# Dividing attention's sums dim-major: sums and denominators moved by DMA instead of turned on TensorE

## The chip, the cores and the metric

The kernel runs on one core of a Trainium2 chip. The metric is the device time of one execution, in microseconds. Lower is better.

## What is computed

Two transformer layers on a sequence of 1024 tokens with 256 dims, in float32. Each layer adds attention with 16 heads of 16 dims to x, and then a gated feed-forward network (FFN). Layer 0 has biases and an ALiBi term in attention and an FFN of 704 hidden units, layer 1 an FFN of 768 hidden units on weights rounded to float8.

```
def attn(x, Wq, Wk, Wv, Wo):                 # layer 0 adds biases and alibi
    q, k, v = split_heads(x @ Wq), split_heads(x @ Wk), split_heads(x @ Wv)
    p = softmax(causal(q @ k.T / sqrt(16)))
    return join_heads(p @ v) @ Wo
def ffn(x):
    return (silu(x @ Wg) * (x @ Wu)) @ Wd
for layer in (0, 1):
    x = x + attn(layernorm(x))
    x = x + ffn(layernorm(x))
```

## The kernel before

The program is written engine by engine, and each engine's order is fixed by hand; semaphores stand for every dependence. The 1024 tokens are eight tiles of 128 (t = 0 to 7), in two halves (c = 0: tiles 0 to 3, c = 1: tiles 4 to 7). PSUM has eight banks: ring a (banks 0 to 3, emptied by ScalarE) and ring b (banks 4 to 7, emptied by VectorE). The lists of ring jobs (`ring_a_jobs`, `ring_b_jobs`) give each job its bank; a job takes its bank when the job four places before it has been emptied.

Attention handles four heads and one half at a time, a group (g, c) of the list `CGS`; the last three are (2, 1), (3, 1) and (3, 0). `attention_order` is a list that TensorE and VectorE both follow: scores for the row maxima, their reduction on VectorE (L1258), a small turn of the maxima (L815), which VectorE copies to `mT` (L1271) and SP moves to `qS` (L499), and exp steps. In an exp step TensorE computes scores in two pairs of heads (L765), ScalarE takes the exponential into `prob` (L1141), GpSimd zeroes the triangle on the diagonal (L590) and TensorE multiplies with v (`times_v`, L785) one step later. The tile `v1` holds for each head 16 columns of v and 16 columns of ones, so one product yields 16 rows of sums and 16 equal rows of denominators per head, in bank 7. When a group is complete ScalarE copies these 128 rows to `oT` (L1128). The copy for a group stands behind the first exp step of the next.

From there to the output projection Wo, tile by tile: TensorE turns `oT` so that queries are on the partitions (`query_major`, L833), VectorE takes the reciprocal of the 16 denominators of each query and multiplies (`divide`, L1328, L1330), TensorE turns the result back (`dim_major`, L839), ScalarE copies it to `onT` (L1176), TensorE multiplies by Wo (`times_wo`, L845), and VectorE adds the result to x (L1246) and takes the statistics of the layer norm (L1222, L1224). Tiles 4 and 5 (`EARLY`) pass these steps inside the last four exp steps, two tiles in one instruction on VectorE (L1358 to L1366). Tiles 6, 7, 0, 1, 2, 3 (`RING`) follow behind attention, with stages of three tiles overlapped.

GpSimd computes the reciprocal deviation of a pair of tiles (`rstd_of`, L599, L601) and normalises tiles 4 to 7 itself (L605); VectorE normalises tiles 0 to 3 (L1233). TensorE turns the normalised tiles (L689) and ScalarE copies them to `xnT` (L1051; in layer 1 to a pair of float16 tiles, with a subtraction on VectorE, L1338). The FFN begins with tiles 4 to 7: for each hidden tile ht a gate and an up product (L916 in layer 0, L921 in layer 1), silu on ScalarE (L1190), and the hidden product on VectorE (L1392; in layer 1 L1398, and a remainder L1347 for a three-way split). Tiles 0 to 3 are turned behind hidden tile `TURNS_BEHIND` of the first half. Layer 0 ends its hidden units with a rest pair (L930), then come the down products (L944).

In the FFN of layer 0 the weights of layer 1's FFN are loaded one after the other into the space of `oT` (GpSimd's queue, L640). VectorE masks them (`round_w8`, L1242, at ht == 2 of each half), and GpSimd rounds them (L553 to L558). SP's queue also spreads the parts of q and k before attention (L493).

Of the kernel before, what the change touches and what calls it, by code (L numbers as in the profile page):

```python
# [89 lines left out]
TURNS_BEHIND = (2, 3)  # L90
# [3 lines left out]
XN_BASE = (0, NT, NT + TPC, 2 * NT + TPC)  # L94


EARLY = (4, 5)
RING = (6, 7, 0, 1, 2, 3)
E_STEPS = {(1, 1): ["on"], (2, 2): ["turn"], (3, 2): ["wo"]}
E_JOBS = [job for at in sorted(E_STEPS) for job in E_STEPS[at]]  # L100


def e_banks(L, kind):

    first = B_AT["on", L, RING[0]] % 4
    on = 4 + first
    return slice(on, on + len(EARLY)) if kind == "on" else 15 - on - (on + 1)


def ring_a_jobs():  # L110

    jobs = []
    for L in range(LAYERS):
# [19 lines left out]
def ring_b_jobs():  # L133

    jobs = []
    for L in range(LAYERS):
# [7 lines left out]
        for n in range(len(RING) + 2):  # L144
            if n < len(RING):
                jobs.append(("on", L, RING[n]))
            if n >= 2:
                jobs.append(("wo", L, RING[n - 2]))
            if n == len(RING) - 1:
                jobs += turns[0:TPC]  # L150
        jobs += ups[0:TURNS_BEHIND[L]] + turns[TPC:] + ups[TURNS_BEHIND[L]:]
# [150 lines left out]
def two_layer_kernel(nc, a, out, tail):  # L302
    with ExitStack() as ctx:
# [132 lines left out]
        def e_made(L, kind):  # L436

            return L * len(E_JOBS) + E_JOBS.index(kind) + 1

        def e_left(engine, L, kind):  # L440

            engine.wait_ge(e_free, e_made(L, kind))
# [1012 lines left out]
```

## Time and profile before

| | us |
|---|---|
| runs | 437.48, 439.1, 444.05 |
| median of the runs | 439.1 |
| span of the profiled execution | 441.7 |
| TensorE busy in it | 410.0 |
| VectorE busy | 297.1 |
| ScalarE busy | 232.9 |
| GpSimd busy | 170.2 |

The span goes from the first to the last instruction of one profiled execution. Its own time beside the span is not listed apart; of the listed runs, two lie below the span and one above it. Busy times are sums over the span; an engine that waits for a semaphore is not busy.

### The profile page before, as it was taken

To read this page: it belongs to the slowest core of one execution; us is meant where nothing else is said; L and a number is where in the kernel's file an instruction comes from. 1 tells how busy PE (TensorE), PEld (TensorE's weight loads), DVE (VectorE), ACT (ScalarE), POOL (GpSimd) and SP (SyncE) were. 2 spreads that over 40 slices of the span, in tenths; PEclk is the share of its full clock that TensorE was granted. 3 is DMA by queue.
4 is the path that set the end of the run, shared out by engine and by line. 5 is a ranking of instruction groups with operands and counts; after the bars stand their busy time and mean duration, and the time that the engine had idled before them with its cause. 6 is when DMAs were issued, how large, how long until landed. Compare 5 with 4: busy or idle time off the path is not lost.

```text
span 441.7 us, 14528 instructions
## 1 busy us (share of the span) xinstructions
PE 410.0 (93%) x6328; PEld 237.2 (54%) x6328; DVE 297.1 (67%) x596; ACT 232.9 (53%) x377; POOL 170.2 (39%) x250
## 2 busy tenths in 40 slices
PE   5799789999999988999999998998999999888997
PEld 5356564555555347544377466544555553465476
DVE  4636489999998216521336586899999981188883
ACT  3535355577776973221101541655877769635950
POOL 4107013314033144478692000234361544453770
PEclk9989799999999999999999997999999999999999
DMA  6899550000000000200100479400000000000002
GB/s 204 129 239 263 128 148 4 4 3 4 4 2 5 4 1 6 65 8 9 64 0 0 120 200 224 106 5 4 3 4 3 4 5 2 2 1 0 1 26 71
DMA packets 21657, 22.97 MB, mean 52 GB/s; under 512 B 2588, under 2 KB 20858, under 8 KB 21594
## 3 DMA queue, kind: packets, MB, share of 16 engines
q1 hardware_dynamic: 20498, 19.03, 17.8%
q0 software_dynamic: 544, 2.49, 1.9%
q8 instruction: 50, 0.82, 0.8%
q10 hardware_dynamic: 552, 0.53, 0.4%
q14 instruction: 13, 0.11, 0.1%
HBM read 8.27 MB, written 1.05 MB: 21 GB/s over the span
## 4 chain that ended last, share of the span: by engine, by line
PE 71%; DVE 14%; ACT 4%; DMA 3%; issue 3%; POOL 2%; SPq 2%; ACTq 0%; DVEq 0%
PE ps L785 11%; PE ps L765 11%; DVE mx L1258 11%; PE ps L743 10%; PE ps L916 8%; PE ps L1012 5%; PE ps L944 4%; PE ps L921 4%; ACT prob L1141 4%; PE ps L677 4%; PE ps L980 4%; DMA col_rows<-in_L_ffn_up_scale 3%; PE ps L845 3%; PE ps L751 2%; POOL xn L605 1%
## 5 line engine op out<-in xcount | busy, mean ns | idle before, releaser
L1258 DVE TENSOR_REDUCE mx<-ps 128x1 f32<-128x512 f32 (+3 forms) x304 | 181.1, 654 | 28.9 <-PE ps L751 24.1
L1141 ACT ACTIVATE prob<-ps 128x1024 f32<-128x1024 f32 (+1 forms) x192 | 145.4, 812 | 63.4 <-PE ps L765 63.1
L743 PE MATMUL ps<-kS,qS 96*32 96x512 bf16 (+21 forms) x1536 | 111.9, 321 | 4.4 <-DVE mx L1258 3.0
L590 POOL TENSOR_SCALAR_AFFINE_SELECT prob<-prob 128x256 f32<-128x256 f32 x128 | 51.9, 412 | 163.9 <-ACT prob L1141 162.5
L765 PE MATMUL ps<-qS,kS 101*32 101x512 bf16 (+7 forms) x1536 | 95.2, 326 | 3.7 <-ACT prob L1141 3.6
L785 PE MATMUL ps<-prob,v 128*32 128x512 f32 (+3 forms) x768 | 80.1, 489 | 0.6 <-POOL prob L590 0.4
L743 PEld LDWEIGHTS ps<-kS,qS 99*32 99x32 bf16 (+1 forms) x1536 | 42.8, 95 | 50.4 <-DVE mx L1258 28.1
L748 PE MATMUL ps<-mask_q,identb 128*32 128x32 bf16 (+1 forms) x1024 | 51.1, 186 | 2.7 <-issue 2.7
L765 PEld LDWEIGHTS ps<-qS,kS 101*32 101x32 bf16 (+1 forms) x1536 | 35.0, 96 | 31.2 <-ACT prob L1141 15.8
L751 PE MATMUL ps<-mask_q,identb 128*32 128x64 bf16 (+1 forms) x512 | 45.4, 198 | 0.0
L748 PEld LDWEIGHTS ps<-mask_q,identb 128*32 128x32 bf16 x1024 | 28.1, 98 | 14.0 <-issue 9.2
L916 PE MATMUL ps<-xnT,gu0T 128*128 128x512 f32 x80 | 34.7, 593 | 0.0
L751 PEld LDWEIGHTS ps<-mask_q,identb 128*32 128x32 bf16 x512 | 28.8, 99 | 5.9 <-issue 0.4
L916 PEld LDWEIGHTS ps<-xnT,gu0T 128*128 128x128 f32 x80 | 15.1, 190 | 18.3 <-issue 17.9
L785 PEld LDWEIGHTS ps<-prob,v 128*32 128x32 f32 x768 | 19.6, 109 | 9.3 <-POOL prob L590 3.1
L657 POOL TENSOR_TENSOR kS<-prob,qS 128x512 bf16<-128x512 f32 x12 | 18.7, 1563 | 6.6 <-ACT qS L1166 5.6
L921 PE MATMUL ps<-xnT,gu 128*128 128x512 f16 x96 | 21.0, 379 | 0.0
L1051 ACT COPY xnT<-ps 128x256 f32<-128x256 f32 x24 | 7.4, 383 | 25.7 <-PE ps L689 25.6
L1190 ACT ACTIVATE rest<-ps 128x512 f32<-128x512 f32 x10 | 6.0, 597 | 27.0 <-PE ps L916 27.0
L1392 DVE TENSOR_TENSOR qS<-ps,rest 128x512 f32<-128x512 f32 x10 | 6.9, 691 | 18.9 <-PE ps L916 18.8
L944 PE MATMUL ps<-d0T,qS 128*128 128x256 f32 x80 | 18.6, 386 | 0.0
L1246 DVE TENSOR_TENSOR x<-ps,x 128x256 f32<-128x256 f32 x20 | 8.3, 416 | 15.0 <-PE ps L952 10.3
(146 smaller groups left out, 537.0 us busy)
## 6 DMA issues: line engine op xcount, KB each, us to landing
qS<-parts SPq DMA_DIRECT2D x24, 128.0 KB, 3.3
kS<-parts SPq DMA_DIRECT2D x24, 128.0 KB, 3.4
qS<-prob SPq DMA_DIRECT2D x12, 128.0 KB, 8.0
kS<-prob SPq DMA_DIRECT2D x12, 128.0 KB, 7.5
qS<-xn SPq DMA_DIRECT2D x12, 128.0 KB, 3.4
kS<-xn SPq DMA_DIRECT2D x12, 128.0 KB, 2.9
out<-x SPq DMA_DIRECT2D x8, 128.0 KB, 1.7
oT<-in_L_ffn_gate_w POOLq DMA_DIRECT2D x1, 768.0 KB, 4.8
```

The source lines that it names most:

```text
L590: nc.gpsimd.affine_select(out=square, in_=square, compare_op=ALU.is_ge, fill=0.0, base=0, pattern=[[0, 2], [1, P]], channel_multiplier=-1) ...
L743: mmi = nc.tensor.matmul(span[r:r + STRIP, 0:seen], qS[0:K_MAX[L], c, g * G + h, qt * P + r:qt * P + r + STRIP], kS[0:K_MAX[L], g * G + h, ...
L748: mmi = nc.tensor.matmul(span[r:r + STRIP, keys - P + r:keys - P + edge], identb[:, r:r + STRIP], mask_q[:, r:edge], start=False, stop=True)
L751: mmi = nc.tensor.matmul(span[r:r + STRIP, keys - P + r + STRIP:keys], identb[:, r:r + STRIP], mask_q[:, r + STRIP:P], start=True, stop=True)
L765: mmi = nc.tensor.matmul(bank[r:r + STRIP, off:CH], kS[0:K_EXP[L], h, kt * P + r:kt * P + r + STRIP], qS[0:K_EXP[L], c, h, off:CH], start= ...
L785: mmi = nc.tensor.matmul(bank[32 * h:32 * h + 32, off:CH], v1[:, kt, g * G + h, :], prob[:, n % 3, h, off:CH], start=kt == 0, stop=s == LA ...
L916: mmi = nc.tensor.matmul(bank[:, :], gu0T[:, m, j, ht * P:(ht + 1) * P], xnT[:, j, c * CH:(c + 1) * CH], start=j == 0, stop=j == CJ - 1)
L921: mmi = nc.tensor.matmul(bank[:, :], gu1[:, m, j, ht * P:(ht + 1) * P], xhl[:, j, s, c * CH:(c + 1) * CH], start=j + s == 0, stop=j == CJ ...
L944: mmi = nc.tensor.matmul(bank[:, 0:C], fT[:, ht, t * P:(t + 1) * P], d0T[:, ht, :], start=start and ht == 0, stop=stop and ht == WHOLE[0] - 1)
L1012: mmi = nc.tensor.matmul(bank[:, :], attn_w(L, w)[:, j, mt * P:(mt + 1) * P], xnT[:, j, c * CH:(c + 1) * CH], start=j == 0, stop=j == CJ - 1)
L1141: nc.scalar.activation(prob[:, n % 3, 2 * pair:2 * pair + 2, off:CH], ps[:, 2 * (m % 2):2 * (m % 2) + 2, off:CH], ACT.Exp, scale=SCALE).th ...
L1258: ins = nc.vector.tensor_reduce(mx[:, slot, qt, heads[0]:heads[-1] + 1, part], src, AX_X, ALU.max)
```

## The change

The columns of `v1` alternate: v, one, v, one. So the rows of `oT` alternate too: a sum and, below it, its denominator. After each group's copy SP starts two DMAs (`move_o`): the 64 even rows go to `num`, which is `xnT`, with dims on the partitions in the order that Wo needs, and the 64 odd rows to `den`, which is `xn`. Before the first of them SP waits until v and all parts of q and k have been read from these two tiles. VectorE divides there: a reciprocal in place on `den` and a product in place on `num`, in six pieces: `NORMS_EARLY` (dims 0 to 127 of both halves, 512 queries each; dims 128 to 255 of tiles 4, 5 and of tiles 6, 7) behind the last maxima, and `NORMS_LATE` (dims 128 to 255 of tiles 0, 1 and of 2, 3) behind the normalisation of tiles 6, 7. `query_major`, `dim_major`, `onT` and the early jobs go.

Wo takes two tiles into one bank. Tiles 4, 5 and 6, 7 stand behind attention; tiles 0, 1 and 2, 3 stand ahead of hidden tiles 2 and 3 of the FFN's first half (`WO_BEHIND`), and so do their adds and statistics on VectorE, with the normalisation behind the hidden tile's product. VectorE now normalises tiles 6 and 7, GpSimd 4 and 5. The turns of tiles 0 to 3 move to hidden tile 4 (layer 0) and 5 (layer 1). The masks `round_w8` move to hidden tile 4 of the first and 3 of the second half. On GpSimd's queue the first weight load waits for the moved sums and stands ahead of the last `rstd_of`.

```
-TURNS_BEHIND = (2, 3)
+TURNS_BEHIND = (4, 5)
+POOL_TILES = (4, 5)
+WO_PAIRS = ((4, 5), (6, 7), (0, 1), (2, 3))
+WO_BEHIND = {2: (0, 1), 3: (2, 3)}
+ROUND_AT = ((0, 4), (1, 3))
+WIDE = 256
+NORMS_EARLY = [(0, 0, 0, CH), (0, 1, 0, CH), (1, 1, 0, WIDE), (1, 1, WIDE, CH)]
+NORMS_LATE = [(1, 0, 0, WIDE), (1, 0, WIDE, CH)]
...
+        num = xnT
+        den = xn[:, :, :].rearrange("p t i -> p (t i)").rearrange("p (c j q) -> p c j q", c=NC, j=CJ)
...
+            def move_o(L, cg):
+                g, c = CGS[cg]
+                j, half = g * CJ // NG, slice(g % (NG // CJ) * G * HD, (g % (NG // CJ) + 1) * G * HD)
+                sp.wait_ge(o_taken, L * N_CG + cg + 1)
+                for part, dst in enumerate((num[half, j, c * CH:(c + 1) * CH], den[half, c, j, :])):
+                    sp.dma_start(dst, oT[part:P:2, g, c * CH:(c + 1) * CH]).then_inc(o_moved[j][c], 16)
...
                 for cg in range(1, N_CG):
                     spread_max(L, cg)
+                    if cg == 1:
+                        sp.wait_ge(a_full, A_AT["v", L, NT - 1] + 1)
+                        for k in range(N_QK):
+                            sp.wait_ge(stacked[k], 16 * len(Q_PARTS) * (L + 1))
+                    move_o(L, cg - 1)
+                move_o(L, N_CG - 1)
...
-            nc.gpsimd.memset(v1[:, :, :, HD:2 * HD], 1.0).then_inc(ones_v, 1)
+            nc.gpsimd.memset(v1[:, :, :, 1::2], 1.0).then_inc(ones_v, 1)
...
             cut_triangles(0)
             rstd_of(2)
-            rstd_of(3)
-            pool.wait_ge(ffn1s_in, 16)
-            pool.wait_ge(b_full, B_AT["wo", 0, RING[-1]] + 1)
             for n in range(2):
-                if n:
+                if n == 0:
+                    for j in range(CJ):
+                        for c in range(NC):
+                            pool.wait_ge(o_moved[j][c], o_landed(0))
+                else:
                     pool.wait_ge(w8_round, n)
                 pool.dma_start(w8.rearrange(...), w8_src[n]).then_inc(w8_in, 16)
+                if n == 0:
+                    rstd_of(3)
                 pool.wait_ge(w8_exp, n + 1)
...
+            def times_wo(L, pair):
+                bank = take_b(("wo", L, pair))
+                pe.wait_ge(o_normal, L * N_NORM + norms_for(pair))
+                for n, t in enumerate(pair):
+                    for j in range(CJ):
+                        mmi = nc.tensor.matmul(bank[:, n * C:(n + 1) * C], num[:, j, t * P:(t + 1) * P], attn_w(L, 3)[:, j, :],
+                                               start=j == 0, stop=j == CJ - 1)
+                mmi.then_inc(b_full, 1)
             def out_projection(L):
+                pe.wait_ge(m_free, (L + 1) * N_MAX)
+                for pair in WO_PAIRS[0:2]:
+                    times_wo(L, pair)
+                pe.wait_ge(s_free, 2 * (L + 1) * N_STEP)
+                pe.wait_ge(o_taken, (L + 1) * N_CG)
+                ln_transposes("ffnT", 2 * L + 1, FFN_C[0], L, *((take_a, a_full) if L == 0 else (take_b, b_full)))
...
                     for ht in range(WHOLE[L]):
+                        if c == FFN_C[0] and ht in WO_BEHIND:
+                            times_wo(L, WO_BEHIND[ht])
                         if (c, ht) == (FFN_C[0], TURNS_BEHIND[L]):
                             ln_transposes("ffnT", 2 * L + 1, FFN_C[1], L, *ring)
...
-                    nc.scalar.copy(v1[:, t, :, 0:HD], bank[:, 0:C].rearrange("p (h d) -> p h d", h=NH)).then_inc(a_free, 1)
+                    nc.scalar.copy(v1[:, t, :, 0::2], bank[:, 0:C].rearrange("p (h d) -> p h d", h=NH)).then_inc(a_free, 1)
...
+                def divide(norm):
+                    j, c, first, end = norm
+                    dve.wait_ge(o_moved[j][c], o_landed(L))
+                    below, above = den[:, c, j, first:end], num[:, j, c * CH + first:c * CH + end]
+                    chain(nc.vector.reciprocal(below, below))
+                    settle()
+                    nc.vector.tensor_tensor(above, above, below, ALU.mult).then_inc(o_normal, 1)
...
+                for norm in NORMS_EARLY:
+                    divide(norm)
                 if L == 0:
                     dve.wait_ge(x_biased, NT)
+                for pair in WO_PAIRS[0:2]:
+                    add_wo(pair)
+                ln_normalise(2 * L + 1, DVE_TILES[1][0:2])
+                if L == 1:
+                    transposed_half(FFN_C[0])
+                for norm in NORMS_LATE:
+                    divide(norm)
                 for i, c in enumerate(FFN_C):
                     for ht in range(WHOLE[L]):
-                        if L == 0 and ht == 2:
+                        if L == 0 and (i, ht) in ROUND_AT:
                             round_w8(i)
-                        if (i, ht) == (0, 1):
-                            ln_normalise(2 * L + 1, FFN_C[1])
+                        if i == 0 and ht in WO_BEHIND:
+                            add_wo(WO_BEHIND[ht])
...
+                        if i == 0 and ht in WO_BEHIND:
+                            ln_normalise(2 * L + 1, WO_BEHIND[ht])
```

## Rows read from the trace of the kernel before

**Rows 1.** The page, part 1: busy us, share of the span, instructions.

```profile
PE 410.0 (93%) x6328; PEld 237.2 (54%) x6328; DVE 297.1 (67%) x596; ACT 232.9 (53%) x377; POOL 170.2 (39%) x250
```

**Rows 2.** Timeline of VectorE, layer 0's tail: start, us, what, idle before it.

```profile
149.57 0.21 DVE L1271 COPY mT<-ps 32x128 bf16<-32x128 bf16 x1 [0.40 <-PE ps L815]
162.29 0.36 DVE L1358 RECIPROCAL rec<-ps 128x32 f32<-128x32 f32 x1 [12.51 <-PE ps L833]
...
167.72 0.69 DVE L1366 TENSOR_TENSOR x<-ps,x 128x512 f32<-128x512 f32 x1 [2.13 <-PE ps L845]
```

**Rows 3.** Timeline of TensorE, layer 0's tail and first gates.

```profile
161.12 1.06 PE L833 MATMUL ps<-ident,oT 128*128 128x128 f32 x8
...
165.69 1.99 PE L845 MATMUL ps<-w,onT 128*128 128x256 f32 x8
167.61 0.42 PE L785 MATMUL ps<-prob,v 128*32 128x128 f32 x8
...
181.34 7.03 PE L916 MATMUL ps<-xnT,gu0T 128*128 128x512 f32 x16
```

**Rows 4.** Timeline of ScalarE, layer 0's tail.

```profile
160.38 0.59 ACT L1128 COPY oT<-ps 128x512 f32<-128x512 f32 x1
...
179.59 0.37 ACT L1051 COPY xnT<-ps 128x256 f32<-128x256 f32 x1 [0.84 <-PE ps L689]
```

**Rows 5.** Timeline of GpSimd, layer 0's tail and FFN.

```profile
169.71 0.22 POOL L599 TENSOR_SCALAR ve<-mv 128x2 f32<-128x2 f32 x1 [3.30 <-DVE mv L1224]
...
170.84 2.44 POOL L605 TENSOR_SCALAR xn<-x,mv,rstd 128x256 f32<-128x256 f32 x2
...
176.56 2.44 POOL L605 TENSOR_SCALAR xn<-x,mv,rstd 128x256 f32<-128x256 f32 x2
...
190.20 5.39 POOL L553 TENSOR_SCALAR oT<-oT 128x1536 f32<-128x1536 f32 x1 [5.55 <-DVE oT L1242]
```

**Rows 6.** VectorE by line: count, ns minimum/median/maximum; the last also total us, mean ns.

```profile
L1328 DVE RECIPROCAL rec<-ps x12: 223/225/258, 169.5 to 396.1; 128x16 f32<-128x16 f32 x12
...
L1358 DVE RECIPROCAL rec<-ps x2: 358/358/358, 162.3 to 381.5; 128x32 f32<-128x32 f32 x2
...
L1233 DVE TENSOR_SCALAR xn<-x,mv,rstd x24: 399/409/414, 6.1 to 404.4; 128x256 f32<-128x256 f32 x24
...
L1242 DVE TENSOR_SCALAR oT<-oT 128x1536 int32<-128x1536 int32 x2 | 1.9, 959 | 5.6 <-DMA oT<-in_L_ffn_up_w 5.6
```

**Rows 7.** Waits of SP's queue, 60 to 200 us: total us, times, longest.

```profile
SPq L499 <- DVE mT L1271: 82.6, 6, 17.5
```

**Rows 8.** Timeline of SP's queue, layer 1: six issues of 128 KB.

```profile
245.37 4.07 SPq L493 DMA_DIRECT2D qS<-parts  x6
```

**Rows 9.** DMA issues, 160 to 275 us: count, size, median us to landing.

```profile
qS<-parts SPq DMA_DIRECT2D x12, 128.0 KB, 2.4
```

**Rows 10.** Timeline of TensorE and of VectorE in layer 0's FFN.

```profile
216.71 3.65 PE L930 MATMUL ps<-xnT,gu0T 128*64 128x512 f32 x16
...
212.78 0.96 DVE L1242 TENSOR_SCALAR oT<-oT 128x1536 int32<-128x1536 int32 x1 [5.56 <-DMA oT<-in_L_ffn_up_w]
```

**Rows 11.** Timeline of TensorE in layer 1's FFN.

```profile
400.60 5.34 PE L921 MATMUL ps<-xnT,gu 128*128 128x512 f16 x24
...
407.22 15.70 PE L921 MATMUL ps<-xnT,gu 128*128 128x512 f16 x72
```

**Rows 12.** Timeline of VectorE in layer 1's FFN.

```profile
404.70 0.75 DVE L1398 SCALAR_TENSOR_TENSOR prob<-ps,cols,rest 128x512 f32<-128x512 f32 x1
...
406.09 0.75 DVE L1398 SCALAR_TENSOR_TENSOR prob<-ps,cols,rest 128x512 f32<-128x512 f32 x1
```

**Rows 13.** Stretches: length, busy us per engine, granted clock (PEclk), DMA share, GB/s.

```profile
48.00:52.00 4.00, 2.21 (x21) 1.89 (x22) 1.29 (x2) 0.40 (x1) 0.00 (x0) 0.58 0.51 127
52.00:56.00 4.00, 4.00 (x47) 2.99 (x49) 1.50 (x3) 1.64 (x5) 0.00 (x0) 0.56 0.02 6
...
170.00:182.00 12.00, 10.69 (x62) 8.67 (x63) 8.39 (x27) 4.90 (x12) 7.46 (x9) 1.00 0.02 6
```

**Rows 14.** Timeline of TensorE at the lower clock, layer 1's first maxima.

```profile
273.05 3.78 PE L677 MATMUL ps<-w1T,xnT 128*128 128x256 f32 x8
```

More of the change, by code:

```diff
@@ L89, with xn_made, norms_for @@
 TURN_ORDER = [t for c in FFN_C for t in range(TPC * c, TPC * (c + 1))]
-TURNS_BEHIND = (2, 3)
+TURNS_BEHIND = (4, 5)
 DOWN_ORDER = ((4, 0, 5, 1, 2, 3, 6, 7), (4, 5, 6, 7, 0, 1, 2, 3))
 LN_PAIRS = ((0, 1, 2, 3), (2, 3, 0, 1), (2, 0, 1, 3), (2, 3, 0, 1))
[L94 to L107, printed above, removed]
+POOL_TILES = (4, 5)
+DVE_TILES = ((0, 1, 2, 3, 4, 5, 6, 7), (6, 7, 0, 1, 2, 3))
+def xn_made(ln, t):
+    before = sum(len(DVE_TILES[n % 2]) for n in range(ln))
+    return before + DVE_TILES[ln % 2].index(t) + 1
+WO_PAIRS = ((4, 5), (6, 7), (0, 1), (2, 3))
[4 more added lines that the diff above has]
+NORMS_LATE = [(1, 0, 0, WIDE), (1, 0, WIDE, CH)]
+N_NORM = len(NORMS_EARLY) + len(NORMS_LATE)
+def norms_for(pair):
+    j, c, first, end = (NORMS_EARLY + NORMS_LATE)[-4 + WO_PAIRS.index(pair)]
+    assert (j, c, first) == (CJ - 1, pair[0] // TPC, pair[0] % TPC * P)
+    return len(NORMS_EARLY) - 2 + WO_PAIRS.index(pair) + 1
 def ring_a_jobs():
@@ L127, in ring_a_jobs @@
         turns = [("ffnT", L, t) for t in TURN_ORDER] if L == 0 else []
-        jobs += [("onT", L, t) for t in RING[:-1]] + turns[0:TPC] + [("onT", L, RING[-1])]
-        jobs += gates[0:TURNS_BEHIND[L]] + turns[TPC:] + gates[TURNS_BEHIND[L]:]
+        jobs += turns[0:TPC] + gates[0:TURNS_BEHIND[L]] + turns[TPC:] + gates[TURNS_BEHIND[L]:]
     return jobs
@@ L143, in ring_b_jobs @@
         turns = [("ffnT", L, t) for t in TURN_ORDER] if L == 1 else []
[L144 to L151, printed above, removed]
+        jobs += [("wo", L, pair) for pair in WO_PAIRS[0:2]] + turns[0:TPC]
+        for n, up in enumerate(ups):
+            if n in WO_BEHIND:
+                jobs.append(("wo", L, WO_BEHIND[n]))
+            if n == TURNS_BEHIND[L]:
+                jobs += turns[TPC:]
+            jobs.append(up)
         jobs += [("down", L, t) for t in DOWN_ORDER[L]]
@@ L434, in two_layer_kernel, with o_landed @@
         N_STEP = len(STEPS)
[L436 to L442, printed above, removed]
+        def o_landed(L):
+            return 16 * 2 * (L + 1) * NG // CJ
         def attn_w(L, m):
@@ L1226, in ln_stats, with ln_normalise @@
                     ins.then_inc(stats_done, 1)
-            def ln_normalise(ln, half):
-                for t in range(TPC * half, TPC * (half + 1)):
+            def ln_normalise(ln, tiles):
+                for t in tiles:
                     if t % 2 == 0:
@@ L1323, in _, with add_wo @@
                 attention(L)
-                def divide(bank, t):
-                    bank = bank.rearrange("p (h d) -> p h d", h=NH)
-                    chain(nc.vector.reciprocal(rec[:, t % 2].unsqueeze(2), bank[:, :, HD:HD + 1]))
-                    settle()
-                    return nc.vector.tensor_tensor(xn[:, t].rearrange("p (h d) -> p h d", h=NH), bank[:, :, 0:HD],
-                                                   rec[:, t % 2].unsqueeze(2).to_broadcast([P, NH, HD]), ALU.mult)
+                def divide(norm):
[3 more added lines that the diff above has]
+                    chain(nc.vector.reciprocal(below, below))
+                    settle()
+                    nc.vector.tensor_tensor(above, above, below, ALU.mult).then_inc(o_normal, 1)
+                def add_wo(pair):
+                    bank = bank_b(("wo", L, pair))
+                    tiles = slice(pair[0], pair[-1] + 1)
+                    nc.vector.tensor_tensor(x[:, tiles], bank.rearrange("p (t i) -> p t i", t=len(pair)), x[:, tiles],
+                                            ALU.add).then_inc(b_free, 1)
+                    dve.wait_ge(b_free, B_AT["wo", L, pair] + 1)
+                    for t in pair:
+                        ln_stats(t)
                 def transposed_half(half):
```

145 lines of the change are left out of this document (21 added, 124 removed).

## Prediction

> **What bounds the kernel now.** I began with the page's busy line: TensorE is busy for 93% of the span [rows 1], so a stretch in which TensorE works without a gap can only grow when work is put into it, and a gain has to come from the stretches in which it waits. The change touches one such stretch in each layer, the passage from attention to the first gate matmul, so I read the timeline of each engine there. In layer 0 VectorE has turned its last maxima at 149.78 and idles 12.51 us [rows 2]. TensorE does the Wo product of the early tiles (165.69 to 167.68) and then the last product with v (to 168.03); the first gate matmul starts at 181.34 [rows 3]. The 13.3 us between are a chain over four engines: turn, divide, turn, copy, Wo, add, statistics, normalise, turn, copy. TensorE, VectorE, ScalarE and GpSimd each wait in it, and none sets it alone. Layer 1 repeats it 219.26 us later (181.34 against 400.60) [rows 3, 11]. Behind it, layer 0's FFN is bound by TensorE: gates from 181.34, the rest pair from 216.71 to 220.36 [rows 3, 10]. In layer 1's FFN 72 matmuls take 15.70 us, nine hidden tiles at 1.74 us [rows 11], while VectorE needs 1.39 us for the two steps of one (404.70 to 406.09) [rows 12]. So there VectorE has 0.35 us to spare per hidden tile, and no more.
>
> All times below are in the frame of that one execution. Its span is 441.7 us; the listed runs are 437.48, 439.1 and 444.05, and the median lies 2.6 us under the span. I add the difference worked out here to the median.
>
> **What the change adds.** The divisor now stands once per head and dim, so 2 x 256 x 1024 divisors per layer lie in four tiles of 128x512, and VectorE takes the reciprocal of 2048 elements per partition per layer. Before it took 8 x 16 = 128. The price: 16 elements took 225 ns and 32 took 358 ns [rows 6], so 133 ns for 16 more, 8.3 ns each. From there 512 cost 225 + 496 x 8.3 = 4.34 us and 256 cost 2.22 us. The multiply behind it is 0.69 us for 512 [rows 2] and about 0.41 for 256 (the normalise of that width) [rows 6]. A wide division is 5.1 us with its gap, a narrow one 2.65.
>
> The lower bound of the unknown is 0.7 us for a wide reciprocal, if the elements streamed at the 0.6 to 1.3 ns of the other operations (959 ns for 1536, 0.69 us for 512) [rows 2, 6]; the upper is the slope. I take the slope, since both of its points are reciprocals. They read PSUM, though, and the new ones read SBUF. The Trainium skill, "VectorE: DVE Perf Modes", section "First, the fixed hardware budget", says that Reciprocal is an iterative divide with a repeat count of 8; this agrees with the slope and speaks against the change. The same page's section "The perf-mode tier table" lists two fp32 elements per cycle for single-source operations from SBUF; whether a reciprocal has that mode no row shows.
>
> The 16 transfers per layer of 128 KB cost nothing outside the last: a move waits for a group's sums, which are copied early in the next group, and the row maxima queued behind it on SP are due at that group's end; SP now waits 82.6 us in six such waits [rows 7]. The strided ones in v1 change no instruction count, and I price them at nothing; they are written ahead of attention.
>
> **The chain in layer 0, anew.** VectorE divides dims 0 to 127 of both halves in its idle time: 149.8 + 2 x 5.1 = 160.0. The next division needs group (3, 1), whose sums are copied from 160.38 to 160.97 [rows 4]. SP issues two transfers at 0.68 us each (six in 4.07) [rows 8] and one lands 2.4 us after its issue [rows 9]: 161.65 + 2.4 = 164.1. VectorE's cover ends at 160.0, so it waits 4 us. Tiles 4, 5 are divided at 166.8 and tiles 6, 7 at 169.4. TensorE has done its last product with v by then: the 1.99 us of early Wo right in front of it are gone [rows 3], as are the early turns, so it ends by 166. Eight matmuls of Wo are 1.99 us: tiles 4, 5 from 166.9 to 168.9, tiles 6, 7 from 169.5 to 171.5.
>
> The adds come behind all four divisions. Add and statistics of a pair take 1.99 us until GpSimd starts (167.72 to 169.71) [rows 2, 5], its variance step 1.13 (to 170.84), its two normalisations 2.44 [rows 5]. So tiles 4, 5 go 169.5, 171.5, 172.6, 175.05. Tiles 6, 7 have statistics at 173.5, but GpSimd is free only at 175.1: 176.2, then VectorE's two normalisations (0.41 each) [rows 6] to 177.0. From the end of a normalisation to the end of the copy of its turned tile it was 0.96 us (179.00 to 179.96) [rows 4, 5]. The gates start at 178.0, which is 3.3 us earlier than 181.34.
>
> **What comes back in layer 0.** The FFN to the end of the rest pair was 39.0 us (181.34 to 220.36) without gaps. Two pairs of Wo now stand in it: +4.0, and TensorE has nothing to hide them. The turns of tiles 0 to 3 come behind hidden tile 3, whose normalisations wait for that tile's product: +0.8 (0.69 and 0.82, less the turns of the two tiles that are ready). That gives 178.0 + 39.0 + 4.0 + 0.8 = 221.8.
>
> The moved rounding costs a little too. The first mask moves behind hidden tile 3: 178.0 + 4 x 3.5 (16 matmuls, two hidden tiles, in 7.03) [rows 3] + 4.0 + 1.5 + 0.96 = 198.5, where GpSimd started at 190.20 [rows 5], 8.3 later. The second load, for which VectorE waited until 212.78 after 5.56 us of idling [rows 10], lands at 221.1. The waiting instruction now stands ahead of hidden tile 3 of the second half, and TensorE's down product needs the bank that this tile's product frees: 221.1 + 0.96 + 0.75 = 222.8, a stall of 1.0. So the down product starts at 222.8 instead of 220.36: +2.5. GpSimd's second rounding ends later as well; its next norm step may add 0 to 1, kept for the range.
>
> **Layer 1.** The tail is the same; one more VectorE step on the turned tile puts the first gate at 397.6 instead of 400.60. But VectorE now has the late divisions, 2 x 2.65, before its first hidden product: 402.9. Then come, before hidden tile 5: five products and four remainders (5 x 0.79 + 4 x 0.60), two adds with statistics (3.8), two pairs of normalisations (1.6) and four steps on turned tiles (1.7), 13.45 us: 416.35. In the kernel before, TensorE had passed hidden tile 5 at 407.22 + 3 x 1.74 = 412.45. Both then go on at TensorE's 1.74, so nothing is won back: +3.8.
>
> **The clock.** TensorE idles some 5 us of the 6.5 between 171.5 and 178.0. Where it was busy for 2.21 of 4 us the mean granted clock was 0.58, and 0.56 in the next 4 us although it worked without a gap; in the tail of before, busy 10.69 of 12 us, it stayed at 1.00 [rows 13]. At the lower level (1.2 GHz) eight matmuls of 256 columns took 3.78 us [rows 14] instead of 1.99. I expect a fall in both layers. Such a stretch costs half of the work that lies in it, 0 to 3.4 us per layer (0.42 x 4 + 0.44 x 4 = 3.4). In layer 0 I take 2.1, since part of it falls on idle time; in layer 1 0.3, since VectorE holds TensorE up anyway.
>
> **Sum:** 2.5 + 3.8 + 2.1 + 0.3 = +8.7, so 447.8 us, which is 2.0% above 439.1.
>
> **Rivals.** *The reciprocal's price halves where it reads SBUF.* For it: a one-input VectorE step from SBUF took 0.62 ns per element (959 ns for 1536), against 1.35 (691 for 512) with fixed cost when PSUM is read [rows 2, 6]. Against: an iterated step need not have that form. Gates at 176.35, layer 0 +0.85, layer 1 +0.1 (both 1.65 earlier, and 2.1 less in the late divisions), clock 2.4: +3.3, 442.4.
>
> *Not slower: the slope belongs to the strided PSUM read, and the divisions stream at 1.04 ns.* Narrow ones take 0.9, gates start at 175.8 (-5.5); layer 0 +0.2, layer 1 -1.9, clock +2.4: +0.7, 439.8. It decides where a 256-wide reciprocal takes under 1 us.
>
> *Slower still: the clock falls before Wo.* TensorE idles between 166 and 169.5 except for the first pair. If the lower level starts there, the second pair takes 3.8 us instead of 2.0 and delays everything behind it in both layers (2 x 1.9), and the gates of layer 0 and the first hidden tiles of layer 1 run longer at half rate (+1.3, +1.0): 447.8 + 6.1 = 453.9. For it: the pauses of about 1 us there, one after the other. Against: in the tail of before, 1.3 us of idling in 12 left the clock at 1.00 [rows 13].
>
> **How the numbers follow.** Forecast 0.58 (444 to 451), half price 0.12, streaming 0.05, early fall 0.25. The range, 441 to 454.5, leaves out the streaming case and the ends of the others. A difference of 2% (8.8 us) is about what a measurement of this kernel can tell from none, and the forecast sits on it: slower is half of the forecast and most of the early fall, 0.52; same is the other half and the two cheap cases, 0.45; faster needs a gain that no case gives, 0.03.
>
> **What would show it.** Reciprocals of 4.3 and 2.2 us; VectorE idle some 4 us before the third division of each layer; Wo of tiles 6, 7 ending 22 us behind the last turned maxima; the first gate about 3 us earlier, and the down product 2 to 5 us later; in layer 1 TensorE waiting for VectorE in the first six hidden tiles; a granted clock of 0.5 at the first gates. Wrong it would be if the reciprocal is cheap, if the clock stays up, or if the late divisions find cover that I did not see.

## The result and the profile after

The change makes the kernel slower: 453.95 us, median of six runs (450.21 to 455.9), against 438.17 (435.93 to 444.05). The ratio is 1.035, with a 95% interval of 1.029 to 1.041. The forecast was 447.8 in a range of 441 to 454.5. Of all the runs below one stood apart at a lower clock, 454.16 us with all Wo pairs in front, and that kernel's median and ratio leave it out.

Single executions of the same code differ by several us. In the nine traces of the changed kernel and its variants, which differ only behind that point, the last maxima of layer 0 were turned between 142.91 and 147.75 us after the start. The four late ones (from 145.46) had a granted clock of 0.58 to 0.67 between 48 and 52 us, the five early ones (to 144.48) had 1.00 there. The trace of before, with 0.58 [rows 13], turned them at 149.57, the latest of all. So I compare stretches between events: last turned maxima, first gate matmul, first down matmul of each layer. What the change costs ahead of the last maxima they do not show. This view counts stretches of the kernel before: length, busy us of TensorE, its weight loads, VectorE, ScalarE and GpSimd, granted clock, DMA share, GB/s. In each layer the first line runs from the last maxima to the first gate and the second from there to the down product.

```profile
149.57:181.34 31.77, 27.95 (x313) 16.66 (x305) 11.86 (x35) 18.20 (x33) 14.08 (x26) 1.00 0.02 4
181.34:220.30 38.96, 38.96 (x106) 16.93 (x104) 11.45 (x21) 7.77 (x15) 26.02 (x11) 1.00 0.13 41
368.82:400.60 31.78, 28.03 (x312) 16.60 (x305) 13.29 (x39) 18.21 (x33) 14.13 (x26) 1.00 0.01 2
400.60:422.76 22.16, 21.82 (x105) 10.26 (x104) 18.99 (x34) 19.03 (x36) 14.11 (x11) 1.00 0.00 1
```

The same four of the changed kernel:

```profile
144.48:174.94 30.46, 21.09 (x249) 9.89 (x241) 18.21 (x22) 16.28 (x27) 11.73 (x23) 0.91 0.09 26
174.94:221.43 46.49, 45.14 (x120) 20.94 (x121) 15.85 (x30) 7.37 (x15) 20.49 (x11) 0.95 0.09 31
368.74:397.22 28.48, 19.64 (x249) 8.72 (x242) 18.53 (x26) 16.27 (x27) 10.99 (x22) 0.96 0.06 20
397.22:429.53 32.31, 28.94 (x120) 14.26 (x121) 27.47 (x43) 19.02 (x36) 13.84 (x13) 0.88 0.00 1
```

The gates come 1.31 and 3.30 us earlier after the maxima, and the FFN up to the down product takes 7.53 and 10.15 us longer: 137.74 against 124.67 us, +13.07. Behind layer 1's down product the two traces agree within 0.1 us; between the layers the changed one is 1.2 us shorter. The last column but two shows the other difference: the clock was 1.00 in all four stretches and is now below 1 in each.

The page's first part, to set beside [rows 1]: TensorE's share falls to 90%, VectorE's rises from 67 to 72.

```profile
PE 403.2 (90%) x6232; PEld 227.9 (51%) x6232; DVE 322.6 (72%) x588; ACT 229.6 (51%) x365; POOL 164.6 (37%) x246
```

VectorE's timeline, layer 0, in answer to [rows 2]:

```profile
144.74 3.35 DVE L1288 RECIPROCAL xn<-xn 128x512 f32<-128x512 f32 x1
...
160.09 1.75 DVE L1288 RECIPROCAL xn<-xn 128x256 f32<-128x256 f32 x1 [7.22 <-DMA xn<-oT]
...
166.14 0.69 DVE L1296 TENSOR_TENSOR x<-ps,x 128x512 f32<-128x512 f32 x1 [1.72 <-PE ps L853]
...
172.74 0.82 DVE L1191 TENSOR_SCALAR xn<-x,mv,rstd 128x256 f32<-128x256 f32 x2 [2.92 <-POOL rstd L618]
```

TensorE's timeline, layer 0, in answer to [rows 3]:

```profile
160.18 0.43 PE L804 MATMUL ps<-prob,v 128*32 128x128 f32 x8 [0.51 <-POOL prob L607]
162.45 5.38 PE L853 MATMUL ps<-w,xnT 128*128 128x256 f32 x16 [1.84 <-DVE xnT L1290]
170.64 0.41 PE L708 MATMUL ps<-ident,xn 128*128 128x128 f32 x2 [2.82 <-POOL xn L622]
...
174.94 9.46 PE L883 MATMUL ps<-xnT,gu0T 128*128 128x512 f32 x16 [0.55 <-ACT xnT L1018]
```

The chain that was worked out can be followed: divisions, Wo, adds, GpSimd's step, turns, gates. Two groups are longer than their work: 16 matmuls of Wo take 5.38 us where eight took 1.99 [rows 3], and the first 16 gates 9.46 against 7.03. The stretches, as in [rows 13], say why. TensorE was busy for 0.43 us of 2, and the lower level stood from about 162.6 to 166; after the pauses of 168 to 174 it stood again, below the first gates:

```profile
160.00:162.00 2.00, 0.43 (x8) 0.16 (x8) 1.88 (x2) 1.31 (x2) 0.13 (x1) 1.00 0.00 0
162.00:164.00 2.00, 1.55 (x4) 1.32 (x5) 1.97 (x3) 0.76 (x2) 0.00 (x0) 0.66 0.40 133
164.00:166.00 2.00, 2.00 (x6) 1.55 (x6) 0.42 (x1) 0.00 (x0) 0.00 (x0) 0.50 0.09 29
...
174.00:176.00 2.00, 1.45 (x4) 0.58 (x3) 1.97 (x3) 0.74 (x2) 0.00 (x0) 0.50 0.88 264
176.00:178.00 2.00, 2.00 (x4) 0.93 (x3) 1.76 (x2) 0.00 (x0) 0.00 (x0) 0.50 0.31 129
```

TensorE in layer 1, in answer to [rows 11]:

```profile
385.86 1.97 PE L853 MATMUL ps<-w1T,xnT 128*128 128x256 f32 x8 [1.00 <-DVE xnT L1290]
...
397.22 5.74 PE L888 MATMUL ps<-xnT,gu 128*128 128x512 f16 x16 [1.08 <-DVE xnT L1308]
...
413.42 0.41 PE L708 MATMUL ps<-ident,xn 128*128 128x128 f32 x2 [1.39 <-DVE xn L1191]
415.81 0.69 PE L708 MATMUL ps<-ident,xn 128*128 128x128 f32 x2 [1.98 <-DVEq L1353]
416.29 13.41 PE L888 MATMUL ps<-xnT,gu 128*128 128x512 f16 x56
```

Here Wo ran at full speed in this execution, and the first gates did not. TensorE stands still for 3.4 us at the turns of tiles 2 and 3, for VectorE's normalisation and then for the bank of hidden tile 4. VectorE around it, in answer to [rows 12], and GpSimd at the same time:

```profile
412.04 2.39 DVE L1191 TENSOR_SCALAR xn<-x,mv,rstd 128x256 f32<-128x256 f32 x2 [0.39 <-POOL rstd L618]
...
419.38 0.75 DVE L1349 SCALAR_TENSOR_TENSOR prob<-ps,cols,rest 128x512 f32<-128x512 f32 x1 [1.54 <-PE ps L888]
```

```profile
411.97 2.31 POOL L676 TENSOR_TENSOR kS<-prob,qS 128x512 bf16<-128x512 f32 x2
```

The two normalisations took 2.39 us where two took 0.82 in layer 0.

### The profile page after: what moved, and what is told of

Read it like the earlier page. It is cut to its first block, busy times and chain, and to the rows that moved or that the text cites. A ratio compares the mean times of both kernels' runs of the same rounds, so it can differ in the third digit from the quotient of the medians.

```text
span 448.5 us, 14321 instructions
## 1 busy us (share of the span) xinstructions
PE 403.2 (90%) x6232; PEld 227.9 (51%) x6232; DVE 322.6 (72%) x588; ACT 229.6 (51%) x365; POOL 164.6 (37%) x246
## 3 DMA queue, kind: packets, MB, share of 16 engines
HBM read 8.27 MB, written 1.05 MB: 21 GB/s over the span
## 4 chain that ended last, share of the span: by engine, by line
PE 61%; DVE 16%; POOL 7%; DMA 6%; ACT 4%; issue 3%; SPq 2%; DVEq 0%; ACTq 0%; POOLq 0%
DVE mx L1216 11%; PE ps L784 10%; PE ps L804 10%; PE ps L762 9%; PE ps L979 5%; PE ps L888 4%; PE ps L911 4%; PE ps L883 4%; PE ps L947 4%; ACT prob L1108 3%; PE ps L696 3%; DMA col_rows<-in_L_ffn_up_scale 3%; PE ps L853 2%; DMA xn<-oT 1%; PE ps L770 1%
## 5 line engine op out<-in xcount | busy, mean ns | idle before, releaser
L762 PE MATMUL ps<-kS,qS 96*32 96x512 bf16 (+20 forms) x1536 | 111.0, 319 | 4.5 <-DVE mx L1216 3.0
L770 PE MATMUL ps<-mask_q,identb 128*32 128x96 bf16 (+1 forms) x512 | 45.2, 197 | 0.0
L883 PE MATMUL ps<-xnT,gu0T 128*128 128x512 f32 x80 | 37.4, 626 | 0.6 <-ACT xnT L1018 0.6
L1288 DVE RECIPROCAL xn<-xn 128x256 f32<-128x256 f32 (+1 forms) x12 | 27.3, 2278 | 13.7 <-DMA xn<-oT 13.6
L883 PEld LDWEIGHTS ps<-xnT,gu0T 128*128 128x128 f32 x80 | 16.0, 202 | 19.7 <-issue 18.6
L888 PE MATMUL ps<-xnT,gu 128*128 128x512 f16 x96 | 24.7, 420 | 1.1 <-DVE xnT L1308 1.1
L616 POOL TENSOR_SCALAR ve<-mv 128x2 f32<-128x2 f32 x16 | 3.6, 227 | 54.0 <-DVE mv L1182 53.9
L708 PE MATMUL ps<-ident,xn 128*128 128x128 f32 x64 | 11.0, 300 | 13.3 <-POOL xn L622 6.9
```

The lines of the kernel that those rows point to most:

```text
L762: mmi = nc.tensor.matmul(span[r:r + STRIP, 0:seen], qS[0:K_MAX[L], c, g * G + h, qt * P + r:qt * P + r + STRIP], kS[0:K_MAX[L], g * G + h, ...
L770: mmi = nc.tensor.matmul(span[r:r + STRIP, keys - P + r + STRIP:keys], identb[:, r:r + STRIP], mask_q[:, r + STRIP:P], start=True, stop=True)
L883: mmi = nc.tensor.matmul(bank[:, :], gu0T[:, m, j, ht * P:(ht + 1) * P], xnT[:, j, c * CH:(c + 1) * CH], start=j == 0, stop=j == CJ - 1)
L888: mmi = nc.tensor.matmul(bank[:, :], gu1[:, m, j, ht * P:(ht + 1) * P], xhl[:, j, c, s, :], start=j + s == 0, stop=j == CJ - 1 and s == 1)
L1288: chain(nc.vector.reciprocal(below, below))
```

## Experiments

Each ratio is to runs of the kernel before that were taken with the experiment; their medians were 437.23 us for the first four and 438.43 for the others.

**Without the reciprocals.** All twelve reciprocals are left out, the transfers, multiplies and waits stay.

```
-                    chain(nc.vector.reciprocal(below, below))
-                    settle()
```

> The changed kernel with the six reciprocals of each layer left out, so the sums are multiplied by the denominators; everything else stays. The two narrow reciprocals ahead of Wo of tiles 6, 7 are 1.75 us each and the two late ones too. Theory (Wo inside the FFN and falls of the clock make the loss, the divisions little): the gates come some 3 us earlier in each layer, the FFN stretches stay at about 46 and 32 us, and the whole gains 3 to 6 us: 448 to 451. Rival (VectorE's divisions make the loss): most of the 15.8 us go, 442 or less, and layer 1's FFN is back at 24 us or less. Second rival (the transfers of the last groups make it): nothing changes, 454, because VectorE waits for them anyway.

450.23 us (448.77 to 451.28), ratio to before 1.028 (1.023 to 1.034). This interval overlaps that of the changed kernel, so I read the gain from the stretches. They sum to 134.41 us, 3.33 less than in the changed kernel; 3.40 of it is layer 0's passage to the first gate (27.06 against 30.46). Layer 1's passage gained only 0.68 us, where some 3 were expected, and its FFN took 1.05 longer. Its stretch from gate to down, and VectorE's first hidden product in it:

```profile
395.91:429.27 33.36, 29.99 (x120) 14.58 (x121) 23.53 (x41) 19.37 (x36) 13.90 (x13) 0.85 0.00 1
```

```profile
399.52 0.75 DVE L1347 SCALAR_TENSOR_TENSOR prob<-ps,cols,rest 128x512 f32<-128x512 f32 x1 [3.09 <-PE ps L888]
```

VectorE had 3.5 us less to do ahead of this product, and then waited 3.09 us for the first gates, which ran at the lower level. So at the clock that this execution had, the two late reciprocals of layer 1 cost nothing. The kernel is still slower than before, by 9.74 us in the stretches: reciprocals that cost nothing would not save the change, so its loss is not mainly their price. With the divisions gone TensorE had no pause ahead of Wo, and the clock stayed up there; it still fell at the turns and first gates of both layers, and in layer 1 again behind the turns of tiles 2 and 3.

**Dummy matmuls in TensorE's pauses.** They write a bank that nobody uses yet, 28 before Wo, 42 behind its two pairs and 14 behind the turns of tiles 4 and 5; no other work changes its order.

```
+            def keep_warm(L, n):
+                spare = (A_AT["ffnT", L, TPC * FFN_C[0] + TPC - 1] if L == 0 else A_AT["gate", L, FFN_C[0], 3]) % 4
+                for _n in range(n):
+                    nc.tensor.matmul(ps[:, spare, 0:P], identb[:], mask_q[:], start=True, stop=True)
...
+                pe.wait_ge(s_free, 2 * (L + 1) * N_STEP)
+                keep_warm(L, 28)
                 for pair in WO_PAIRS[0:2]:
                     times_wo(L, pair)
-                pe.wait_ge(s_free, 2 * (L + 1) * N_STEP)
+                keep_warm(L, 42)
```

> The changed kernel with small bfloat16 matmuls of 128 columns in TensorE's pauses between attention and the gates (28 ahead of Wo, 42 behind it, 14 behind each of the first two turned tiles), whose results nobody reads. Theory (the lower clock costs 5 to 8 us: in the changed trace Wo took 5.4 instead of 4.0 us, layer 0's first two hidden tiles 9.5 instead of 7.0, layer 1's 5.7 instead of 3.6): the granted clock stays at 1.00 over both tails and the time falls to 446 to 449. Rival (the clock falls only where TensorE waits for others anyway): 453 to 455, with the clock up and the FFN stretches as long as before.

446.01 us (444.24 to 450.07), ratio 1.020 (1.013 to 1.027) against 1.035 of the changed kernel. The stretches with their clock:

```profile
143.73:172.45 28.72, 24.95 (x346) 14.09 (x339) 18.05 (x22) 16.28 (x27) 11.74 (x23) 1.00 0.10 27
172.45:216.71 44.26, 42.78 (x121) 20.02 (x121) 16.12 (x30) 7.38 (x15) 20.50 (x11) 1.00 0.09 33
364.78:393.41 28.63, 24.45 (x347) 14.14 (x339) 18.32 (x26) 16.23 (x27) 11.02 (x22) 1.00 0.06 20
393.41:424.81 31.40, 27.14 (x120) 13.74 (x121) 26.85 (x43) 19.38 (x36) 13.84 (x13) 0.95 0.00 1
```

They sum to 133.01, 4.73 less than in the changed kernel, 3.97 of it in layer 0. TensorE's first gates and VectorE's product of hidden tile 5 in layer 1, and TensorE's turns of tiles 2 and 3:

```profile
393.41 3.61 PE L898 MATMUL ps<-xnT,gu 128*128 128x512 f16 x16 [1.09 <-DVE xnT L1318]
...
408.38 0.41 PE L708 MATMUL ps<-ident,xn 128*128 128x128 f32 x2 [2.29 <-DVE xn L1201]
410.76 0.44 PE L708 MATMUL ps<-ident,xn 128*128 128x128 f32 x2 [1.97 <-DVEq L1363]
```

```profile
414.25 0.75 DVE L1359 SCALAR_TENSOR_TENSOR prob<-ps,cols,rest 128x512 f32<-128x512 f32 x1 [1.46 <-PE ps L898]
```

In the last stretch the clock was still down for a while, behind the standing still at the turns of tiles 2 and 3 (0.95 over 31.40 us, so up to 1.6 us of it). Between 6.7 and 8.34 us over before are therefore not the clock. TensorE's busy time holds 12.27 us of dummies here; without them its work is 107.1 us against 116.75 before. So the change does take 9.7 us of work from TensorE, and the time in which TensorE does none of the kernel's work grows from 7.9 to 26.0 us: by 12.7 us in the two passages and by 5.4 in the two FFNs.

**The masks where they were.** The masks of the weight rounding go back to hidden tile 2 of each half; all else is the changed kernel.

```
-ROUND_AT = ((0, 4), (1, 3))
+ROUND_AT = ((0, 2), (1, 2))
```

> The changed kernel with the masks of the next weights at hidden tile 2 of each half, where they stood in the kernel before. Theory (they cost the 0.4 us by which TensorE waits at the end of layer 0's gates): 453 to 454, and the down product of layer 0 starts without a wait. Rival (the masks moved behind hidden tile 4 hold up layer 0's FFN, which grew by 7.5 us): 449 or less.

461.76 us (456.65 to 462.23), ratio 1.051 (1.042 to 1.060), some 8 us slower than the changed kernel, which none of my theories had. Layer 0 from gates to down takes 54.88 us against 46.49:

```profile
176.31:231.19 54.88, 47.03 (x121) 21.73 (x121) 23.83 (x30) 7.96 (x15) 31.57 (x13) 0.89 0.08 26
```

TensorE stands still for 7.9 us of it (1.4 in the changed kernel), and the clock is lower (0.89 for 0.95). VectorE's and GpSimd's timelines show why:

```profile
196.95 7.89 DVE L1191 TENSOR_SCALAR xn<-x,mv,rstd 128x256 f32<-128x256 f32 x2
```

```profile
195.78 5.40 POOL L570 TENSOR_SCALAR oT<-oT 128x1536 f32<-128x1536 f32 x1
201.26 3.42 POOL L571 TENSOR_TENSOR oT<-oT 128x1536 f32<-128x1536 f32 x1
```

With the earlier mask GpSimd's rounding begins at 195.78, and the two normalisations of tiles 2 and 3, 0.74 us in the changed kernel, take 7.89. The first took 4.38 us and ended at 201.33, just behind GpSimd's first instruction (201.18); the second ended at 204.84, just behind GpSimd's second (204.68). GpSimd's own times are those of before (5.39 in [rows 5]). VectorE was held until a GpSimd instruction ended, one normalisation at a time. The Trainium skill, "SBUF — State Buffer", section "SBUF: two separate sides", calls the port pair that the two engines share "an exclusive lock, not a bandwidth split"; these rows agree, and so do the two normalisations of 2.39 us above, which ended at 414.43, 0.15 behind GpSimd's pair.

**All four Wo pairs ahead of the turns.** The late divisions and pairs leave the hidden tiles and stand in front of the first turn; VectorE normalises tiles 0 to 3 together behind hidden tile 1.

```
-WO_BEHIND = {2: (0, 1), 3: (2, 3)}
+WO_BEHIND = {}
...
-        jobs += [("wo", L, pair) for pair in WO_PAIRS[0:2]] + turns[0:TPC]
+        jobs += [("wo", L, pair) for pair in WO_PAIRS] + turns[0:TPC]
```

> The changed kernel with all four pairs of Wo ahead of the turns, so that they fill TensorE's pause; the late divisions and the adds move ahead of the first hidden product with them. Theory (each pair inside the FFN costs its full 2.0 us, and the pause lets the clock fall): layer 0's FFN stretch goes from 46.5 to 39 to 41 us, the gates come 2 to 4 us later in each layer, the clock falls less, and the whole gains 3 to 7 us: 447 to 451. Rival (Wo inside the FFN is hidden and other things lengthen it): the FFN stretch stays above 44 us and the time rises by what the gates come later, 456 to 461.

449.26 us, median of three runs (444.96 to 450.13), ratio 1.024 (1.015 to 1.032); the interval overlaps that of the changed kernel. Gates to down takes nearly what it took before (38.96, 22.16):

```profile
178.21:218.13 39.92, 39.11 (x105) 17.04 (x105) 9.77 (x18) 7.24 (x15) 19.55 (x9) 1.00 0.06 20
401.43:424.29 22.86, 21.97 (x105) 10.14 (x106) 17.77 (x29) 18.94 (x36) 13.17 (x9) 1.00 0.00 1
```

The passage to the gates takes 34.69 and 35.09 instead of 30.46 and 28.48; layer 1's 6.6 us are more than the 2 to 4 expected. All in all 132.56 us, 5.18 less than in the changed kernel. The clock fell to 0.90 in both passages and was 1.00 behind the gates, where the changed kernel had 0.95 and 0.88. How much of the 5.18 is the place of the pairs and how much is where the clock fell, this run doesn't separate.

**The turns of tiles 0 to 3 in two pieces.** In layer 1 alone, to see whether TensorE's order or VectorE's queue makes the 3.4 us of standing still.

```
-TURNS_BEHIND = (4, 5)
+TURNS_AT = ({4: (0, 1, 2, 3)}, {4: (0, 1), 5: (2, 3)})
```

> In layer 1 the turns of tiles 0 and 1 move ahead of hidden tile 4 and those of tiles 2 and 3 stay ahead of hidden tile 5; nothing else changes. Theory: the 3.4 us for which TensorE waits at these turns (1.39 and 1.98) are the late normalisation of tiles 2 and 3 with an empty queue in front of it; with eight matmuls of hidden tile 4 (1.74 us) between the two pairs, the stretch from the first gate to the down product shrinks from 32.31 to about 30.6, and the time from 450 to about 448.5. Rival: VectorE's own queue sets this stretch (two late divisions, adds, statistics, normalisations and steps on turned tiles are 13 us before hidden tile 5), so the order on TensorE changes nothing: 32.3 again, 450.

455.51 us (452.8 to 456.21), ratio 1.038 (1.031 to 1.045); first gate to down 32.24 us against 32.31. The theory fell and the rival held: hidden tile 4 ran earlier and the wait stood behind it, since the normalisation of tiles 2 and 3 took 2.40 us again. This execution also had the lower level under both layers' early Wo, so that the last maxima to the first gate of layer 1 took 30.01 us instead of 28.48.

**Split turns and dummies.**

> The split turns of layer 1 together with the dummy matmuls that keep TensorE's clock up. Theory: the two gains are in different places and add up: 446.0 less 1.7 is about 444.3, layer 1 from the first gate to the down product 29.7 instead of 31.4. Rival (VectorE's queue sets layer 1 when the clock is up): 446.0 and 31.4.

448.57 us (444.25 to 449.09), ratio 1.022 (1.015 to 1.029); layer 1 from gate to down 31.58 us. The clock was up until the turns and fell behind them (0.89 over the stretch, 0.95 without the split). Up to the end of the turns the split saved 0.18 us (17.45 from the first gate, against 17.63). Again the rival: with the clock up, too, the order on TensorE changes next to nothing in layer 1.

**All pairs in front, and dummies.** The pairs in front as above, with 28 dummies ahead of the first pair, 64 between the second and the third, 28 behind the fourth and 14 behind the turns of tiles 4 and 5.

> All four Wo pairs ahead of the turns, as in the run that had them there, and dummy matmuls in TensorE's pauses (before the first pair, between the second and the third, behind the fourth and behind two of the turns). Theory: of what the changed kernel loses, the clock and the two Wo pairs among the hidden tiles are the two large parts, so that without both it comes down to what the pause before the late pairs costs: layer 0 from the last turned maxima to the down product 70.5 us in the kernel before, here 71 to 73; layer 1 from maxima to down 54 to 55 against 53.9 in the kernel before; the time 437 to 441, within 1% of the kernel before. Rival: the pairs cost the same wherever they stand and the clock was all: 446, as with the dummy matmuls alone.

447.17 us (445.39 to 451.54), ratio 1.023 (1.015 to 1.030). It is the rival's time, not the theory's. Layer 0 took 75.47 us from maxima to down and layer 1 58.94, where 71 to 73 and 54 to 55 were expected; the clock was 1.00 in all four stretches. With the pairs in front, the passages take 35.47 and 36.08 us at a clock of 1.00 and took 34.69 and 35.09 at 0.90. TensorE's timeline in layer 0, first with the dummies, then without them:

```profile
176.56 1.97 PE L855 MATMUL ps<-w,xnT 128*128 128x256 f32 x8 [0.16 <-DVE xnT L1302]
178.36 1.73 PE L863 MATMUL ps<-mask_q,identb 128*128 128x128 bf16 x28
179.93 0.39 PE L708 MATMUL ps<-ident,xn 128*128 128x128 f32 x2
180.15 0.94 PE L863 MATMUL ps<-mask_q,identb 128*128 128x128 bf16 x14
...
183.16 13.97 PE L895 MATMUL ps<-xnT,gu0T 128*128 128x512 f32 x32 [0.61 <-ACT xnT L1030]
```

```profile
176.45 1.04 PE L708 MATMUL ps<-ident,xn 128*128 128x128 f32 x8
178.21 13.97 PE L883 MATMUL ps<-xnT,gu0T 128*128 128x512 f32 x32 [0.73 <-ACT xnT L1018]
```

From the fourth pair to the last turn TensorE waited for no other engine. GpSimd had normalised its two tiles by 173.82 and VectorE its two by 177.07, so the dummies themselves held up the turns. So this run doesn't show whether the two gains add up. An estimate from the rows: with the turns right behind the fourth pair, as in the run without dummies, layer 0's first gate would come 1.76 us behind 178.36, some 3.0 us earlier than it did; in layer 1, where VectorE's last statistics ended at 404.91 and its four steps on turned tiles took 1.40 us, some 1.5. That would make 72.4 us in layer 0, as the theory had it, 57.4 in layer 1, which is more than it had, and still about 5 over before. No run tests it.

**The same, and the masks where they were.**

> The same, and both masks of the weight rounding back to hidden tile 2 of each half. In this order VectorE's four normalisations of tiles 0 to 3 stand behind hidden tile 1, ahead of the first mask, so that GpSimd's rounding begins when they are done. Theory: what made the masks cost 7.8 us there was VectorE's normalisation running beside GpSimd's rounding (7.89 us for two tiles), so here they cost nothing, and the second load lands earlier: 0 to 1.5 us faster than the run with the masks late, each normalisation pair at 0.7 to 0.8 us. Rival: the mask's place itself was the cost (VectorE's queue stands while it waits for the load, and hidden products behind it are late): again some 5 to 8 us slower.

449.02 us (445.75 to 450.09), ratio 1.024 (1.018 to 1.031); the two runs can't be told apart by time. The stretches can:

```profile
143.63:179.02 35.39, 30.93 (x412) 19.75 (x405) 24.31 (x35) 16.17 (x27) 13.68 (x27) 1.00 0.12 41
179.02:218.06 39.04, 39.04 (x105) 17.01 (x105) 10.04 (x16) 7.77 (x15) 23.10 (x7) 1.00 0.07 21
366.29:402.20 35.91, 30.93 (x412) 19.74 (x405) 25.91 (x39) 16.18 (x27) 12.99 (x26) 1.00 0.05 16
402.20:425.06 22.86, 21.97 (x104) 10.15 (x105) 17.75 (x29) 18.96 (x36) 13.15 (x9) 1.00 0.00 1
```

```profile
186.97 1.38 DVE L1203 TENSOR_SCALAR xn<-x,mv,rstd 128x256 f32<-128x256 f32 x4
```

Layer 0 from gates to down is 39.04 instead of 40.00, TensorE busy throughout. The normalisations stand ahead of the mask in this order, four in 1.38 us, and the masks cost nothing. So the 8 us of the run with the masks back were the meeting with GpSimd and the slower clock behind it, not the mask's place. The dummies behind the fourth pair delay the gates here, too. No version of the change came under the kernel before.

## Why the prediction was right, and where it was off

The direction and the mechanism were right: TensorE is relieved, the passage to the gates shortens, and the FFN behind it gives back more. The time, 453.95, lies in the range but beside the likeliest case (444 to 451) and at the place of the rival "the clock falls before Wo" (453.9). Of that rival's condition the profiled execution met half: layer 0's Wo ran at the lower level, layer 1's did not; in the run with split turns both did. That the range held is partly luck. It held by 0.55 us; the rise was 15.8 us over the median of six runs where 8.7 were forecast, and two terms below were too small.

Step by step, with the run that had the clock up in the middle:

| step | forecast | clock up | as changed |
|---|---|---|---|
| layer 0, maxima to first gate | -3.3 | -3.05 | -1.31 |
| layer 0, gate to down | +5.8 | +5.30 | +7.53 |
| layer 1, maxima to first gate | -3.0 | -3.15 | -3.30 |
| layer 1, gate to down | +6.8 | +9.24 | +10.15 |
| sum of these | +6.3 | +8.34 | +13.07 |
| clock, on top | +2.4 | | (in the rows above) |
| sum | +8.7 | | +13.07 |

*Reciprocals.* 3.35 and 1.75 us instead of 4.34 and 2.22. From 256 to 512 elements that is (3351 - 1734) / 256 = 6.3 ns each, between the slope taken (8.3) and the bound; the "half price" rival wanted 2.17 and 1.1. The working let the price decide too much: its streaming case, with divisions of 0.9 us, came to +0.7, but without any reciprocal the stretches were still 9.74 us over before.

*Landing.* From the end of the copy of group (3, 1) (155.89) to the division it was 4.2 us in layer 0 and 3.35 in layer 1, forecast 3.1. So VectorE idled 7.22 and 6.38 us there, not 4: the two wide divisions ended 2 us sooner and the sums landed later. The later landing and the cheaper reciprocals nearly cancel, so the first gates came where they were expected, once the clock is taken out (-3.05 and -3.15 for -3.3 and -3.0).

*What comes back in layer 0.* The sum was right, 5.30 us with the clock up for 5.8, and its terms nearly so. On TensorE each pair held up the gates by 1.72 us (179.40 to 181.12, 184.56 to 186.28), so 3.4 for 4.0. The turns took 2.13 (189.72 to 191.85) where they had taken 0.87 before (188.21 to 189.08), so 1.3 for 0.8. The wait for the late mask ahead of the down product was 0.51 for 1.0, and 0.39 in the changed kernel. That the late masks also keep GpSimd away from VectorE's normalisations was missed; without it the change would have cost some 8 us more.

*Layer 1.* This term was too small: 9.24 us with the clock up, or 7.6 without the clock's share, for 6.8. VectorE was to reach hidden tile 5's product 18.75 us behind the first gate; with the clock up it took 20.84 (393.41 to 414.25). The late divisions were cheaper (4.24 us, not 5.3). But the normalisation of tiles 2 and 3 took 2.40 us instead of 0.8 beside GpSimd, VectorE waited 0.9 us for GpSimd's deviations, and then 1.46 us for the first gates of tile 5, because TensorE could turn the tiles only when VectorE had emptied the bank of tile 4. I had VectorE's queue run without a gap; two waits that go back and forth between the engines were not in the sum. Up to 1.6 us of the 9.24 is the clock behind that wait, a fall that I hadn't forecast. Nor did the late divisions hold layer 1 up as the sum had it: at the clock of the changed kernel they were covered by the slow first gates, as the run without reciprocals shows.

*The clock.* This term, too, was too small, by half or more: 2.4 for 4.7 (as changed less clock up) to 6.3 (with the 1.6 that stayed). In layer 0 the gates lost 2.4 us (9.46 against 7.03) and Wo 1.4 (5.38 against 3.98): the fall before Wo, held to be unlikely because 1.3 us of idling in 12 had left the clock at 1.00 [rows 13], came behind a pause of 1.84 us and a sparse end of attention. In layer 1 the dummies won back only 0.76 us: the first 16 gates take 5.74 us as changed and 3.61 with the clock up, but TensorE then waits for VectorE in either case, as argued.

*Slips in the working.* Four tiles of 128x512 hold 256 x 1024 divisors per layer, not 2 x 256 x 1024, and 416.35 less 412.45 is 3.9, not 3.8. Neither changes the forecast by more than 0.1 us.

*What is open.* The difference of the medians is 15.8 us. The traces show 11.9: the 13.07, less the 1.2 between the layers. The changed kernel's trace is of the fastest of its six runs (450.21). The trace with split turns, 6.0 us longer, shows three ways in which an execution gets longer: later last maxima in layer 0 (3.27 us), the fall before layer 1's Wo (1.53), and 1.17 between the layers. Which of them the other five executions had is not on record; their mean clock, 0.954 to 0.969, was lower than the 0.973 of the trace in each.

## What to carry to other kernels

Taking work from a busy engine pays only if the chain that replaces it has as few gaps as the work had: here TensorE lost 9.7 us of work and gained 18 of waiting, because a transfer, a division and a normalisation now stand in a row. Nearly 19 us of work left the two passages, and they became 6 us shorter; each pair that moved into layer 0's FFN cost its full 1.72 us there. Price a new pause on TensorE twice, once for itself and once for the slower work behind it, and test that with dummy matmuls before anything else is moved. The dummies must end before the work that they bridge to is ready, or they become the delay, as they did behind the fourth pair. When an engine's work is shifted in time, look at what the other engine on its port does then; two instructions of 0.4 us became 7.9 that way.

## What the runs showed of the hardware

A one-input VectorE operation from SBUF to SBUF (128x256, float32) went from 0.41 us [rows 6] to 4.38 and 3.58 us beside GpSimd's rounding, ending 0.15 and 0.16 us behind a GpSimd instruction that had begun before it, while GpSimd kept its 5.40 us.

A reciprocal of float32 in SBUF took 1.73 to 1.75 us for 256 and 3.34 to 3.35 for 512 elements per partition, 6.3 ns for each further element.

In the changed kernel TensorE's granted clock fell to 0.50 behind pauses of only 1 to 3 us. In layer 0 a pause of 1.84 us stood ahead of Wo; 1.00 us at the same place of layer 1 left the clock at 1.00 in the changed kernel's trace and not in that with split turns (16 matmuls of Wo in 5.38 us). In the run with dummies in these pauses it stayed at 1.00 through both passages.
